# A two-pass graph sum on one core: single loads of table positions, 33 one-hots on ScalarE, and other places for the tail slots

## What is computed

```python
def sage_conv(x, edge_index, W_l, b_l, W_r, num_segments):
    src, dst = (edge_index[0], edge_index[1])
    agg = jax.ops.segment_sum(x[src], dst, num_segments=num_segments)
    return agg @ W_l.T + b_l + x @ W_r.T
h = jax.nn.relu(sage_conv(x, edge_index, W_l_in, b_l_in, W_r_in, n))
out = sage_conv(h, edge_index, W_l_out, b_l_out, W_r_out, n)
x = _layernorm(x + out)                 # then the attention layer, not touched
```

## Time and profile before

| what | value |
|---|---|
| median of three runs | 3997.3 us (3989.62 to 3998.96) |
| the profiled execution, its own time | 4001.15 us |
| its span, first to last instruction | 3999.3 us |
| PE, DVE, ACT, POOL busy share of the span | 71%, 68%, 62%, 66% |
| granted TensorE clock, mean | 0.807 |
| HBM read and written | 355.50 and 175.09 MB |

### The profile page before, as it was taken

How to read it: one execution, slowest core, us unless ns; L and a number is a source line. 1 busy time by engine, 2 the same in 40 slices (tenths; PEclk the granted TensorE clock), 3 DMA queues, 4 the chain that set the end, 5 groups by cost and what they waited for, 6 DMA issues and landing times. The chain is left out here.

```text
span 3999.3 us, 82215 instructions
## 1 busy us (share of the span) xinstructions
PE 2838.4 (71%) x28125; PEld 2379.6 (60%) x28125; DVE 2714.7 (68%) x7548; ACT 2490.8 (62%) x7102; POOL 2638.2 (66%) x2669
## 2 busy tenths in 40 slices
PE   3688788887888888874567666676666666667646
PEld 2566566664777777764456655565555665656644
DVE  7898766774455455562467777777876777777776
ACT  4566666775666566630167766787666776677745
POOL 3466765774655565427777777777777777777735
PEclk9999989998999999985567776677776777677767
DMA  3677875113666676723333333333333333333311
GB/s 88 237 284 312 315 313 213 21 20 118 223 232 234 222 237 222 237 92 69 76 77 87 90 85 76 87 94 86 85 82 78 93 87 83 79 82 88 89 31 39
DMA packets 285952, 536.14 MB, mean 134 GB/s; under 512 B 116631, under 2 KB 203217, under 8 KB 278902
## 3 DMA queue, kind: packets, MB, share of 16 engines
q1 hardware_dynamic: 200032, 452.07, 32.7%
q0 software_dynamic: 80256, 76.21, 10.2%
q10 hardware_dynamic: 5246, 2.56, 0.2%
HBM read 355.50 MB, written 175.09 MB: 133 GB/s over the span
## 5 line engine op out<-in xcount | busy, mean ns | idle before, releaser
L2034 POOL DMA_INDIRECT scratch<-fs_scratch,src_idx x728 | 728.8, 1001 | 222.0 <-issue 221.4
L892 POOL DMA_INDIRECT gath<-x_parts,src_idx x532 | 538.8, 1013 | 316.6 <-issue 191.5
L949 ACT ACTIVATE scratch<-sum_x_ps_c 128x600 int32<-128x600 f32 (+5 forms) x690 | 520.0, 770 | 311.2 <-PE sum_x_ps_c L981 266.6
L1066 DVE TENSOR_SCALAR e_tab<-scratch,e_tab 128x700 bf16<-128x700 f16 (+8 forms) x1380 | 526.1, 423 | 257.8 <-PE sum_y_ps_c L981 226.5
L892 POOL DMA_INDIRECT gath<-y_parts,src_idx x412 | 406.6, 987 | 291.6 <-issue 121.0
L2162 ACT ACTIVATE scratch<-scratch,bias,weight 128x32 f32<-128x32 f32 x1360 | 483.7, 399 | 77.2 <-DVE bias L2232 77.2
L2076 PEld LDWEIGHTS ps_e<-fdw,scratch 128*128 128x128 f32 x3136 | 494.3, 239 | 23.2
L2243 DVE SCALAR_TENSOR_TENSOR scratch<-ps_e,attn_sb 128x128 f32<-128x128 f32 x784 | 189.4, 284 | 429.0 <-PE ps_e L2076 427.8
L2076 PE MATMUL ps_e<-fdw,scratch 128*128 128x66 f32 x3136 | 478.0, 319 | 0.0
L949 ACT ACTIVATE scratch<-sum_y_ps_c 128x700 int32<-128x700 f32 (+2 forms) x348 | 280.1, 832 | 279.7 <-PE sum_y_ps_c L981 274.5
L1006 PEld LDWEIGHTS sum_x_ps_d<-parts,scratch 128*128 128x128 f16 x7400 | 383.3, 101 | 102.3 <-ACT scratch L949 44.4
(11 more groups left out here) (363 smaller groups left out, 6241.3 us busy)
## 6 DMA issues: line engine op xcount, KB each, us to landing
count_scratch<-scratch SPq DMA_DIRECT2D x48, 3200.0 KB
scratch<-count_scratch SPq DMA_DIRECT2D x192, 800.0 KB
onehot<-rel_scratch SPq DMA_DIRECT2D x196, 256.0 KB
scratch<-in_edge_attr_2x SPq DMA_DIRECT2D x390, 128.0 KB
fdw<-fd_scratch SPq DMA_DIRECT2D x392, 33.0 KB
scratch<-fs_scratch,src_idx POOLq DMA_INDIRECT x728
gath<-x_parts,src_idx POOLq DMA_INDIRECT x532
gath<-y_parts,src_idx POOLq DMA_INDIRECT x412
```

What stands on the lines that cost most here:

```text
L892: pool.indirect_dma_start(out=rows_in(s, t), out_offset=None, in_=table_dram, in_offset=bass.IndirectOffsetOnAxis(ap=src_idx[:, g, k:k + 1 ...
L949: act.activation(to, ps_c[u % pairs][:, :, 0:q].rearrange("p h (d a) -> p h a d", d=d), ACT.Copy).then_inc(kept, 1)
L1066: d = dve.tensor_scalar(cells[:, n % RING, i * width:(i + 1) * width], count_up[:, 0:width], head_key[:, tile:tile + 1], head_weight[:, ti ...
L2034: pool.indirect_dma_start(out=rows_of(m)[:, t, :], out_offset=None, in_=fs_dram, in_offset=bass.IndirectOffsetOnAxis(ap=src_idx[:, g, k:k ...
```

## The change

Three edits, all in `segment_sum_pass` and its plan.

1. The positions in `table_a` are loaded one register at a time, two loads for each slot directly ahead of the wait for its sums, where one load of up to eight stood ahead of every fourth slot. This holds for both passes.
2. In `sum_x` the one-hots of the first 33 slots (`slots // 2`) are made by ScalarE; VectorE makes the other 34 as before.
3. A step of `sum_x` weighs the longer of two estimates: TensorE's, with 44 ns for a product where it was 66, and VectorE's, 350 ns and 0.26 ns a column for each tile. The slots' tiles, and with them the one-hots, additions and loads, move to other steps.

```diff
         for step in range(len(self.weight)):
             for _, _, length in self.products.get(step, ()):
-                self.weight[step] += 66.0 * ALL_HIGHS / length
+                self.weight[step] += 44.0 * ALL_HIGHS / length
+            unit = head.units[step]
+            made = len(unit["banks"]) / unit["pieces"] * (350.0 + 0.26 * unit["pairs"] * ALL_HIGHS)
+            self.weight[step] = max(self.weight[step], made)
...
-            lent, pairs = slots if read else 0, 2
+            lent, pairs = slots if read else slots // 2, 2
...
                         for i in adds.get(step, ()):
-                            if i % SLOTS == 0:
-                                last = min(G, (n0 + i + SLOTS) * SG)
-                                starts = nc.values_load_multi_w_load_instructions(
-                                    win[0:1, (n0 + i) * SG:last], engines=DVE_ENGINE, min_val=0, max_val=N,
-                                    skip_runtime_bounds_check_because=CLAMPED)[1]
+                            at = (n0 + i) * SG
+                            starts = [nc.values_load_multi_w_load_instructions(
+                                win[0:1, at + g:at + g + 1], engines=DVE_ENGINE, min_val=0, max_val=N,
+                                skip_runtime_bounds_check_because=CLAMPED)[1][0] for g in range(SG)]
...
-                                    to = table_a[rows, bass.ds(starts[i % SLOTS * SG + g], WINDOW)]
+                                    to = table_a[rows, bass.ds(starts[g], WINDOW)]
```

More of the change, by code:

```diff
@@ L1075, in _ @@
                         dve.wait_ge(numbered, 1)
-                    made, starts, heads_added, tails_added = plan.first_item, [], 0, 0
+                    made, heads_added, tails_added = plan.first_item, 0, 0
                     if not lent:
```

## The result

The change made the kernel slower: 4008.2 us (median of six runs, 4005.4 to 4016.5) against 3987.7 for the kernel before in the same set (3984.5 to 3999.0). The ratio is 1.0046, 95% interval 1.0029 to 1.0062. The forecast was 3969 and the range ended at 4004. The sign and nearly the time are those of rival 2, slower by 16 us; measured were 20.5.

The account below looks back on a forecast made before the run. VectorE's time before 381 us and its lumps up to 668 were taken to set the first pass's end. Stretch terms summed to -36; 8 given back for waits no longer hidden made -28, 3969 us, range 3943 to 4004.

Parts of the forecast that it names:

- rival 2: Copies of counts, 102 to 500 us: ScalarE's one-hot blocks become the bound; ends at +16, 4013 us; chance 0.17.
- the sum for TensorE: First pass, 181 to 522 us: blocks at 8.8 us plus gaps give 93, 102 and 136 us, each setting its stretch.
- the gaps: TensorE's waits behind ScalarE's one-hot blocks: 2 to 3 us each, with 1.7 us of slow clock for half of them.
- Working ahead: First pass, against rival 2: VectorE makes cells ahead for two to four units, so its time overlaps the gaps.
- VectorE's relief: First pass: 33 one-hots leave VectorE, 1.15 us each.
- the first 440 us no shorter: Sign of rival 2 in the first pass, together with TensorE's waits for ScalarE over 100 us.
- over 100 us: Sign of rival 2: TensorE's waits for ScalarE in the first pass exceed 100 us.
- near 90%: Sign that the forecast is right: ScalarE near 90% in the stretches from 181 to 381 us.
- The loads: Position loads before slot sums: a pair idles VectorE 0.7 us a slot; without lumps, 522 to 668 us gains 19 us.
- rival 1: Position loads in the storing stretch: single loads stretch too, 1.05 us each, so splitting wins nothing; 3992 us; chance 0.18.
- the estimate of 23 us worse: Position loads up to 668 us: by the 600 ns floor, 46 slots x 0.5 us lost if no cover is left.
- The second pass: TensorE and ScalarE set the pace, so the split loads cost 0 (0 to +5) us.

Follow-up runs that it names:

- nine-block run: The change with nine unbroken one-hots on ScalarE instead of 33, all begun in the first two stretches: 3953.0 us, ratio 0.9898 to the kernel before.
- idle blocks: The change with all one-hots on VectorE and 32 ScalarE blocks into a tile nobody reads: 3999.7 us, ratio 0.9994 to the kernel before.
- pieces: The change with its ScalarE one-hots cut into two Squares or half a Relu beside a slot's tiles: 3959.2 us, ratio 0.9905 to the kernel before.
- the doubled store: The kernel before with counts stored from the upper 64 partitions only, sent twice: one run, 4203.5 us, for the loads alone.

## Why the prediction was wrong

The eight stretches (us, by profile, from copy to copy) against their terms. "Loads, weights" is the run without one-hots on ScalarE, less before; "one-hots" is the change less that run.

| pairs | before | predicted | measured | loads, weights | one-hots |
|---|---|---|---|---|---|
| 1 | 22.8 | +1 | +4.3 | +1.3 | +3.0 |
| 2 | 78.5 | -4 | +0.1 | +2.0 | -1.9 |
| 3 | 99.5 | -6 | +8.5 | -6.7 | +15.2 |
| 4 | 100.7 | -1 | +20.5 | -4.8 | +25.3 |
| 5 | 141.4 | -5 | +6.0 | -11.0 | +17.0 |
| 6 | 145.8 | -19 | -16.7 | -16.6 | -0.1 |
| 7, 8 | 260.9 | -2 | -5.7 | -5.8 | +0.1 |

*The step that failed* is the sum for TensorE in the three stretches from 181 to 522, in the first of them "TensorE 8 x 8.8 + 7 x 3.3 = 93. So 93". Of three engines' sums I took the largest. Two of them were right: VectorE's 83 and 82 us for the third and fourth stretch were 81.5 and 77.7, ScalarE's 88 and 91 were 89.7 and 89.6 (rows of the result). TensorE's 93 and 102 were to be the longest and were, but too small. It was busy 79.5 and 91.3 us where 70 and 79 were forecast, and waited for copies 26.7 and 26.4 us where the gaps were to be 23 and 22. That makes 106 of the 108.0 us, and 118 of the 121.2. In the fifth, 147.4 where its 136 stood, it was busy 116.1 (114 forecast) and waited 26.1 for copies (22). From 183.8 to 413 us its waits and VectorE's read:

```profile
PE sum_x_ps_c L984 <- ACT scratch L952: 45.2, 31, 3.7
...
DVE table_a L1107 <- PE sum_x_ps_c L1022: 30.4, 15, 4.5
DVE e_tab L1069 <- PE sum_x_ps_c L984: 22.9, 29, 2.7
...
PE sum_x_ps_d L1009 <- ACT scratch L952: 7.9, 4, 3.8
...
PE sum_x_ps_c L984 <- DVE e_tab L1069: 2.9, 3, 1.2
```

and without blocks, in the same two stretches of the nine-block run (182.8 to 369.6):

```profile
PE sum_x_ps_c L984 <- DVE e_tab L1069: 18.8, 23, 2.3
...
PE sum_x_ps_c L984 <- ACT scratch L952: 6.9, 9, 1.5
PE sum_x_ps_d L1009 <- DVE scratch L1095: 6.1, 9, 1.3
```

*What a block cost.* Sixteen blocks run in the two stretches, eight in each; the sum had seven in the third, but the block that begins at the last step of the second runs behind that step's copy. TensorE's waits for copies rose from 6.9 to 53.1 us, 2.9 a block. Its busy time for as many matmuls rose from 151.7 to 170.8 us, 1.2 a block: the clock, which is 1.00 and 0.98 without blocks and 0.89 and 0.87 with them. Together 4.1 us, where the sum had 3.3 and 2.8; I had given only half of the gaps the slow clock, and left out the waits for copies that are there without blocks. Rival 2's 101 and 113 us mean 4.4 and 4.2 a block. The stretches grew by less, 42.4 us or 2.7 a block, since TensorE's other waits, for VectorE's cells and sums above all, fell by 23 us: that much did overlap. The idle blocks and the pieces show the cause: occupation in one piece, not the amount of work.

*Working ahead* was my argument against rival 2: "VectorE can make cells ahead for two to four units, so its time overlaps the gaps". VectorE did stand still in them, for two reasons that the rows above show. Its queue is in order, and a block's addition (L1107), which needs TensorE's window, stands in front of the cells: 30.4 us in 15 times. And it may not overwrite cells that TensorE has not counted yet (L1069): 22.9 us in 29 times, 0.4 without blocks. But TensorE then waited only 2.9 us for cells, so by this trace VectorE's standing still is not what set the length. No run tested it; with pieces the wait at L1107 is still 21.2 us, the one at L1069 1.8, and the two stretches take 97.2 and 99.0 us.

*VectorE's relief* was to give 1.15 us a one-hot; with pieces it gave nothing that shows over 33. VectorE was the fullest engine, but its relief shifted the wait to the copies: in the two stretches TensorE's waits for cells fell from 19.8 us (loads and weights) to 10.7 (pieces), and its waits to count for copies (L949 before) rose from 6.2 to 15.5.

*Rival 2's sum* came near partly by luck. Its four stretches from 102 to 522 were to become 37 us longer and became 35.1 longer, but as 0, 8.5, 20.5 and 6 where it has about 16, 4, 12 and 5: from 102 to 181, where VectorE was full, the blocks cost nothing that shows. Its later terms were -21, measured -22.4. Its signs, "the first 440 us no shorter" and waits for ScalarE "over 100 us" (108.8), came, and ScalarE was not near 90% from 181 to 381 but at 83 and 74%.

*The loads* were right in mechanism, and rival 1 is out, although single loads did stretch: 0.90 us at the median, three times what I took. After, the wait in "issue" is 26.7 us over 67 slots, 0.4 a slot (0.7 forecast), and 1.9 at most. The term was mis-sized in the other direction: alone the loads are worth 44 us, not some 23 (the 19 and 4 of rival 1). By the profiles single loads alone took 13.9 us off the sixth stretch, where the sum had 19 for them, 26 off the five ahead of it, where rival 1 puts 4, and 9 off the last two, where it had none: I gave the lumps and the clock back for the sixth stretch only. By the clock records of the two profiles the half clock fell from 96 us in the pass to 37 with single loads; half of the 58 is 29 us. The idle time before the additions fell by 34 there (53.4 to 19.4). Both together are more than the 44; that part of the idle time lay beside other waits would explain it, but is not shown.

The Trainium skill's floor of about 600 ns for a register load ("DMA: Bandwidth & Descriptors", section "Latency and other measured facts") and with it the estimate of 23 us worse did not come about; the trace has 0.30 us for one without stores. That engine and transfer sides never contend, as the Trainium skill has it ("SBUF — State Buffer", section "SBUF: two separate sides"), doesn't describe register loads here, which take three times as long under stores.

*The second pass* was put at 0 with up to 5: 740.7 us before, 736.6 after, and between 736.6 and 744.7 in the profiles of all runs but the doubled store. No difference shows.

## What to carry to other kernels

Work handed to an engine with free time must be cut to what the buffers ahead of its other duty cover: 3.6 us in one piece cost 51 us in all, the same work in pieces of 0.7 us nothing. When you sum up an engine that has to wait for such a piece, give every gap its full length and the slow clock behind it, and keep the waits that it has already. Relief for the fullest engine wins nothing where another wait takes its place. Break up long waits first, and price every one with the clock behind it.

## What the runs showed of the hardware that was not expected

A load of registers from SBUF into VectorE's sequencer took 0.30 us for one register without stores and 0.90 at the median while counts were stored; eight took up to 6.9 us, and 7.8 with the transfer engines 96% busy. With 226 GB/s moved and no such stores, in the second pass, eight took 0.61. TensorE's clock was at 0.50 for 6.8 us, in and behind a gap of 3.6 us in the place shown; over 16 blocks, 2.9 us more of waiting for each came with 1.2 us more of busy time for the same matmuls.
